# Attention with 64-row products issued in pairs, and the maximum carried in row 64

## The reference

```python
x  = tok_emb + pos_emb                          # layer 0: embedding
h  = x + attn0(layernorm(x))                    # softmax(q k^T / 8) x, no value or output weights
h  = h + ffn0(layernorm(h))                     # one of 16 routed experts plus a shared one, two layers
h  = h + attn1(layernorm(h))                    # with biases, value and output weights
h  = h + ffn1(layernorm(h))                     # 8 experts, the 2 best per token, exact gelu
```

## Time and profile before

| | us |
|---|---|
| median of three runs (934.78 to 936.87) | 935.1 |
| the profiled execution | 936.95 |
| its span, first to last instruction | 935.1 |
| PE busy | 891.6 (95%) |
| weight loads busy | 631.5 (68%) |
| DVE, ACT, POOL busy | 603.8, 576.6, 384.1 |

### The profile page before, as it was taken

The page is one execution under the profiler, slowest core; times in us unless marked ns, Lnnn a source line. Parts: engine busy times, 40 slices in busy tenths (PEclk is TensorE's granted clock), DMA queues, the critical chain, the costliest instruction groups (busy, mean ns, idle before and its releaser), DMA issues.

```text
span 935.1 us, 21847 instructions
## 1 busy us (share of the span) xinstructions
PE 891.6 (95%) x6198; PEld 631.5 (68%) x6198; DVE 603.8 (65%) x2610; ACT 576.6 (62%) x1195; POOL 384.1 (41%) x523
## 2 busy tenths in 40 slices
PE   4879999999999999979999999999999999999998
PEld 2657666666766676656666676666777777777775
DVE  5876777778787899967777777774434343434321
ACT  1336666666666666646666666666666666666664
POOL 0133444444437888834444344443333333333300
PEclk9999999999999999989999999999999999999999
DMA  4000000000001222200000000000000000000000
GB/s 103 2 1 2 1 0 0 0 0 0 1 1 49 72 73 68 75 7 1 1 0 0 0 0 1 1 1 7 12 18 11 17 11 17 11 17 11 18 13 23
DMA packets 18995, 15.13 MB, mean 16 GB/s; under 512 B 5762, under 2 KB 18946, under 8 KB 18946
## 3 DMA queue, kind: packets, MB, share of 16 engines
q1 hardware_dynamic: 18946, 14.52, 5.6%
HBM read 10.32 MB, written 4.19 MB: 16 GB/s over the span
## 4 chain that ended last, share of the span: by engine, by line
PE 83%; DVE 12%; issue 2%; ACT 1%; DMA 1%; DVEq 0%; POOL 0%; SPq 0%; ACTq 0%
PE bank L1226 13%; PE bank L1058 13%; PE bank L1206 7%; PE bank L1024 7%; PE bank L1207 6%; PE bank L971 5%; DVE nmax L743 5%; PE bank L1049 5%; PE bank L1050 5%; PE bank L1135 4%; PE bank L996 3%; PE bank L1037 2%; PE bank L1013 2%; PE bank L1014 2%; PE bank L1003 2%
## 5 line engine op out<-in xcount | busy, mean ns | idle before, releaser
L743 DVE TENSOR_REDUCE nmax<-bank 128x1 fp32r<-128x512 f32 x256 | 170.4, 687 | 47.7 <-PE bank L1024 47.5
L360 POOL TENSOR_TENSOR XS<-XN,XS 128x252 fp32r<-128x252 f32 x128 | 98.0, 765 | 211.6 <-ACT XS L402 211.6
L342 POOL TENSOR_TENSOR rstd<-VE,half 128x4 f32<-128x4 f32 x128 | 129.2, 1009 | 119.6 <-DVE VE L661 119.6
L504 ACT ACTIVATE PT<-bank 128x512 f32<-128x512 f32 x256 | 146.0, 596 | 41.8 <-PE bank L1050 35.5
L354 POOL TENSOR_TENSOR XN<-XC,rstd 128x252 f32<-128x252 f32 x128 | 78.3, 612 | 183.9 <-PE bank L1058 183.7
L556 ACT ACTIVATE PT<-bank 128x512 f32<-128x512 f32 x256 | 132.2, 605 | 3.5 <-PE bank L1207 2.8
L475 ACT ACTIVATE OT<-bank 128x256 f32<-128x256 f32 x96 | 36.8, 384 | 154.3 <-PE bank L1058 103.8
L1058 PE MATMUL bank<-PT,XN 128*64 128x256 f32 x1024 | 124.7, 386 | 0.0
L1226 PE MATMUL bank<-PT,W 128*64 128x256 f32 x1024 | 124.5, 386 | 0.0
L1024 PE MATMUL bank<-X,QH 128*128 128x512 f32 x256 | 108.2, 424 | 8.6 <-DVE nmax L743 1.7
L1049 PE MATMUL bank<-QH,X 128*128 128x512 f32 x256 | 113.1, 442 | 0.5 <-ACT Q L497 0.5
(11 more groups left out here) (136 smaller groups left out, 1506.4 us busy)
## 6 DMA issues: line engine op xcount, KB each, us to landing
WR<-experts SPq DMA_DIRECT2D x64, 129.0 KB, 2.0
out<-H SPq DMA_DIRECT2D x32, 128.0 KB, 1.7
W<-pack SPq DMA_DIRECT2D x5, 252.5 KB, 3.9
W<-pack SPq DMA_DIRECT2D x1, 251.5 KB, 5.1
W<-pack SPq DMA_DIRECT2D x1, 243.0 KB, 5.6
tk<-tokens SPq DMA_DIRECT2D x1, 64.0 KB, 4.4
route_sb<-route SPq DMA_DIRECT2D x1, 0.2 KB
```

The lines of the kernel that those rows point to most:

```text
L342: pl.tensor_tensor(rstd[:, par, :], VE[:, par, :], half[:, :], ALU.pow).then_inc(sigma_done, 1)
L504: sc_.activation(PT[:, par, kt, :], bank[4 + kt % 2][:, :], ACT.Exp, scale=SCALE).then_inc(s.e_ready, 1)
L743: v.tensor_reduce(nmax[:, par, t:t + 1], bank[2 + t % 2][:, :], axis=AX, op=ALU.max, negate=True).then_inc(s.max_ready, 1)
```

## The change

In both attentions the products for the maxima use 64 rows instead of 128: rows 0 to 63 of `QH` against rows 0 to 63 of `X2`. The odd tiles use rows 64 to 127 of `QH` (which holds the projection twice) against a new buffer `XD`, whose rows 64 to 127 are a copy of rows 0 to 63 of `X2`. An even and an odd tile are issued one behind the other (`pair_for_max`). The products with `Q2` are halved in the same way (`low_scores`) and come ahead of those with `QH` (`high_scores`), which stay at 128 rows. Minus the maximum now stands in row 64 of `QH` instead of row 0 of `Q2`; `nmax` is 65 columns wide for that, zero but for the last, `spread_max` writes rows 0 to 64 of bank 0, and the matrices that make the queries have a zero in column 64. ACT fills `XD` behind `X2`, and both are told by one semaphore.

```diff
-            nmax = sb("nmax", [P, 2, NT], F32R)
+            XD = sb("XD", [P, 2, SEQ], F32R)
+            nmax = sb("nmax", [P, 2, NT, D + 1], F32R)
...
-                sc_.activation(X2[:, par, :], bank[0][:, :], ACT.Copy).then_inc(s.x2_ready, 1)
+                ins = sc_.activation(X2[:, par, :], bank[0][:, :], ACT.Copy)
+                if s is a0 or s is a1:
+                    ins = sc_.activation(XD[D:P, par, :], bank[0][0:D, :], ACT.Copy)
+                ins.then_inc(s.x2_ready, 1)
...
-                    sc_.activation(Q2[0:1, par, :], bank[7][0:1, :], ACT.Copy).then_inc(s.m_ready, 1)
+                    sc_.activation(QH[D:D + 1, par, :], bank[0][D:D + 1, :], ACT.Copy).then_inc(s.m_ready, 1)
...
+                def pair_for_max(i, par, t):
+                    if t == 0:
+                        pe.wait_ge(s.qh_ready, i + 1)
+                    if t == 2 or not known(i) or i >= 1:
+                        pe.wait_ge(s.max_ready, i * NT + t)
+                    for own, rows, keys in ((t, slice(0, D), X2), (t + 1, slice(D, P), XD)):
+                        mm(bank[2 + own % 2][:, :], QH[rows, par, own * P:(own + 1) * P], keys[rows, par, :],
+                           start=True, stop=True).then_inc(s.s_ps, 1)
...
                 def spread_max(i, par):
                     pe.wait_ge(s.max_ready, i * NT + NT)
+                    if has(i + 1):
+                        pe.wait_ge(s.x2_ready, i + 2)
...
+                def low_scores(i, par, kt):
+                    pe.wait_ge(s.ql_ready, i + 1)
+                    if kt == 2 or not known(i) or i >= 1:
+                        pe.wait_ge(s.e_ready, i * NT + kt)
+                    for own, rows, keys in ((kt, slice(0, D), X2), (kt + 1, slice(D, P), XD)):
+                        mm(bank[4 + own % 2][:, :], keys[rows, par, own * P:(own + 1) * P], Q2[rows, par, :],
+                           start=True, stop=False)
+                def high_scores(i, par, kt):
+                    pe.wait_ge(s.m_ready, i + 1)
+                    for own in (kt, kt + 1):
+                        mm(bank[4 + own % 2][:, :], X2[:, par, own * P:(own + 1) * P], QH[:, par, :],
+                           start=False, stop=True).then_inc(s.st_ps, 1)
```

More of the change, by code:

```diff
@@ L40 @@
 CENTRE, LOWER, FUSE, FUSED, NORM = 8, 15, 17, 20, 14
-CONSTS = 7
+CONSTS = 8
 HIGHS, LOWS = 5, 6
@@ L333, in _ @@
             pl.memset(f32(XS[:, :, :, 0:1]), 1.0).then_inc(consts_set, 1)
-            pl.memset(f32(XS[:, :, :, D:D + 1]), 0.0).then_inc(consts_set, 1)
+            pl.memset(f32(XS[:, :, :, D:D + 1]), 1.0).then_inc(consts_set, 1)
             pl.memset(R1[:, :], 0.0).then_inc(consts_set, 1)
+            pl.memset(f32(nmax[:, :, :, :]), 0.0).then_inc(consts_set, 1)
             pool.wait_ge(consts_set, CONSTS)
@@ L742, in maxima @@
                         dve.wait_ge(s.s_ps, i * NT + (t + 1))
-                        v.tensor_reduce(nmax[:, par, t:t + 1], bank[2 + t % 2][:, :], axis=AX, op=ALU.max,
+                        v.tensor_reduce(nmax[:, par, t, D:D + 1], bank[2 + t % 2][:, :], axis=AX, op=ALU.max,
                                         negate=True).then_inc(s.max_ready, 1)
@@ L754, in finish @@
                     v.tensor_tensor(hb(i), hb(i), ON[:, :, :], ALU.add).then_inc(s.h_done, 1)
+                maxima(0, 0, range(NT))
                 low_parts(0, 0)
-                maxima(0, 0, range(NT))
                 def body(i, par):
-                    if has(i + 1):
-                        low_parts(i + 1, 1 - par)
-                        maxima(i + 1, 1 - par, range(2))
                     if not known(i) or i >= 1:
@@ L765, in body @@
                     if has(i + 1):
-                        maxima(i + 1, 1 - par, range(2, NT))
+                        maxima(i + 1, 1 - par, range(NT))
+                        low_parts(i + 1, 1 - par)
                     moments_on(s, after, i + 5, 1 - par)
@@ L1014, in project @@
                     mm(bank[1][:, :], AL[:, layer, :], X2[:, par, :], start=False, stop=True).then_inc(s.q_ps, 1)
-                def scores_for_max(i, par, t):
+                def pair_for_max(i, par, t):
                     if t == 0:
                         pe.wait_ge(s.qh_ready, i + 1)
[L1020 to L1025, removed]
+                    if t == 2 or not known(i) or i >= 1:
[3 more added lines that the diff above has]
+                           start=True, stop=True).then_inc(s.s_ps, 1)
@@ L1027, in spread_max @@
                 def spread_max(i, par):
                     pe.wait_ge(s.max_ready, i * NT + NT)
+                    if has(i + 1):
+                        pe.wait_ge(s.x2_ready, i + 2)
+                    else:
+                        pe.wait_ge(after.x2_ready, 1)
                     if known(i) and i == 0:
                         pe.wait_ge(h0_ready if before is None else before.h_done, NSEQ)
-                    if not known(i) or i >= 1:
-                        pe.wait_ge(s.m_ready, i)
@@ L1034, in spread_max @@
-                    if not known(i) or i >= 2:
-                        pe.wait_ge(s.h_done, i - 1)
                     for t in range(NT):
-                        last = mm(bank[7][0:1, t * P:(t + 1) * P], nmax[:, par, t:t + 1],
+                        last = mm(bank[0][0:D + 1, t * P:(t + 1) * P], nmax[:, par, t, :],
                                   IR[:, :], start=True, stop=True)
                     last.then_inc(s.m_ps, 1)
[L1041 to L1050, removed]
+                def low_scores(i, par, kt):
[5 more added lines that the diff above has]
+                           start=True, stop=False)
@@ L1071, in attention @@
                     rest_before()
-                for t in range(NT):
-                    scores_for_max(0, 0, t)
+                for t in (0, 2):
+                    pair_for_max(0, 0, t)
                 def body(i, par, lane):
@@ L1078, in body @@
                         project(i + 1, 1 - par)
[L1079 to L1083, removed]
                     if not known(i) or i >= 1:
                         turn_back(s, before, i - 1, 1 - par)
-                    scores(i, par, 2)
+                    low_scores(i, par, 0)
+                    high_scores(i, par, 0)
                     if has(i + 1):
-                        scores_for_max(i + 1, 1 - par, 1)
-                    scores(i, par, 3)
+                        pair_for_max(i + 1, 1 - par, 0)
+                    turn_on(s, after, i + 2, par)
+                    low_scores(i, par, 2)
+                    high_scores(i, par, 2)
                     if has(i + 1):
-                        scores_for_max(i + 1, 1 - par, 2)
-                        scores_for_max(i + 1, 1 - par, 3)
+                        pair_for_max(i + 1, 1 - par, 2)
                     if not has(i + 1):
@@ L1285, in wide, with once @@
         return np.concatenate([m, m], 1)
+    def once(m):
+        m = wide(m)
+        m[:, D] = 0.0
+        return m
     def led(first, m):
@@ L1291 @@
     none = np.zeros(D, np.float32)
-    put("wq0", wide(led(none, x["L0_attn_Wq"])))
+    put("wq0", once(led(none, x["L0_attn_Wq"])))
     put("wk0", wide(led(none, x["L0_attn_Wk"])))
-    put("wq1", wide(led(x["L1_attn_bq"], x["L1_attn_Wq"])))
+    put("wq1", once(led(x["L1_attn_bq"], x["L1_attn_Wq"])))
     put("wk1", wide(led(x["L1_attn_bk"], x["L1_attn_Wk"])))
@@ L1312 @@
     ct[D, 0] = 1.0
-    put("ct", wide(ct))
+    put("ct", once(ct))
     c0 = np.zeros((P, 2, D + 1), np.float32)
```

## The result

The changed kernel takes 955.2 us (median of four runs, 954.28 to 955.52) against 935.9 us beside it: 1.0205 times the time before, 95% interval 1.0187 to 1.0222. That is 19 us slower where 7 us were forecast. The profiled execution took 955.41 us, its span 953.5 us, 18.4 us more than before.

The account below looks back on a forecast made before the run. PE was taken to bound the attentions, in its own order. Its terms summed to +0.10 us a sequence, +6.4 us for 64; with +1 us, 936.95 became 944.3 us, less 1.85 us: 942 us, range 914 to 970 us.

Parts of the forecast that it names:

- Side by side: Products on two row halves run together on PE, so a pair takes the room of one product, 0.23 us.
- a pair's loads in turn: Rival: a pair's two weight loads follow each other, each pair 0.11 us longer, 28 us more, 970 us; chance 0.12.
- no overlap: Rival: the halves do not run side by side, 0.23 us more a pair, 59 us, 1001 us; chance 0.08.
- Loads hidden behind the other half: Rival: a pair's weights load while the other division streams, four loads of 0.11 us go, 914 us; chance 0.20.
- Nine switches and the loads in the open: On PE, seven more switches, +0.63 us a sequence; six open weight loads, +0.66 us, and two taken at half, +0.10 us.
- The wait for DVE goes: PE's wait for DVE before the last product for the maxima goes, with its open load: -0.37 us a sequence.
- both large terms: The division's switches, loads and saved products, 0.47 us a sequence, and the vanished wait for DVE, -0.37 us.
- Even: no cost by these numbers, but no cover either: At the second low pair, PE arrives as the second exponential ends, 1.65 us after the first high scores start: no wait.
- Together +1 us: First `XD` copy on the path into attention 0, 0.5 us, and each phase's last sequence, 0.3 us each.

Follow-up runs that it names:

- both whole: The changed kernel with all eight products over 128 rows again, its order, pairwise waits and copy into `XD` kept: 941.4 us, 1.0057 of the kernel before.

## Why the prediction was wrong

The direction was right, and so was what the division costs on PE; two other terms were not, and with them the size: 942 us were forecast and 955.2 us measured, inside the range given but with a rise nearly three times the one forecast. By the steps:

- *Side by side.* Right: the starts are within 0.01 us. With it the rivals that need a pair's loads in turn, or no overlap, fall. Loads hidden behind the other half did not show either: the load of each pair starts with its product.
- *Nine switches and the loads in the open.* Right: from a pair to the high scores 0.43 us and between the two high products 0.34 us, as laid out. Undoing the division measured 0.42 us a sequence against the 0.47 us that the switches, loads and saved products came to; the extra product of 64 rows cost 15.8 us more than that of 128, where 15 us were expected.
- *The wait for DVE goes.* Right: the product of the earlier trace rows waits no more. With both whole and its wait taken off a sequence is 6.45 us against 6.76 us before, 0.31 us less, where this term had 0.37 us. So both large terms were some 0.05 us too big, and that their sum, +0.10 us, came out as forecast is in part luck.
- *"Even: no cost by these numbers, but no cover either".* This step failed. The second exponential ended at 202.03, 1.63 us behind the start of the first high scores and nearly as laid out (1.65), but the pair's load started only at 202.14, 0.11 us later; the sum names no time for the way from ACT to PE. PE without a wait would have started the pair 0.20 us behind its last transpose, at 202.08. So the wait is 0.08 us, 5 us in all, near the 6 us at which the prediction had priced 0.1 us more on ACT, and the experiments with whole products showed it growing to 0.39 us as soon as PE comes earlier. A step that comes out even should have been priced with the delay of the signal.
- *"Together +1 us"*, the starts of the two attentions. This failed too: they cost some 6 us: the first two sequences of an attention took 2.8 and 4.4 us more than two later ones, where before it was 0.7 us less and 1.6 us more. The sum takes all 64 sequences at durations of full clock and has nothing for the longer idle time at the starts or for the granted clock there, although it fell to half in the trace before.

Together: 0.10 us x 64 = 6 us as forecast, 0.08 us x 64 = 5 us of waiting, 6 us at the starts, 1 us elsewhere: 18 of the span's 18.4 us.

## What to carry to other kernels

A lone pair of products on half the array's rows was not worth it here: each change between whole and divided costs the switch and a weight load that nothing covers, here 0.25 us for one excursion, more than the 0.23 us that one product of 512 columns takes. Whether a longer run of pairs pays, no run here shows. Before a change in the order of an engine is charged to the operations in it, run the new order with the old operations: here the order alone was a gain, the divided operations and the waits in pairs were the loss, and only their sum was slower. When a layout of waits comes out even, put the signal's delay into it, and look at the granted clock where the pipeline starts.

## What the runs showed of the hardware

- Halves of the rows run side by side like halves of the columns: two products of 64 rows and 512 columns start less than 0.01 us apart, and their weight loads, 128 columns each, run together (0.03 us apart where the pair had waited). The opening load (0.11 us), the columns (0.23 us) and the switch behind them (0.09 us) make 0.43 us.
- The price of a switch is about the same for rows as for columns: into 64 rows 0.08 us (0.38 - 0.30), out of them 0.09 us (0.43 - 0.11 - 0.23), out of column halves 0.09 us. The Trainium skill ("TensorEngine Tiling (Array Packing)", Key Properties) has a change of mode drain the engine and names no price; the runs agree that it costs. Its Theoretical Speedup, up to twice the rate, is what the columns of a pair show, and not what a lone pair takes, 0.43 us against 0.46 us.
- From the end of an activation's record to the start of the weight load that it releases 0.11 us passed (202.03 to 202.14), so in 24 of the 29 sequences of attention 0 past its start that the trace shows whole; in the other five it was 0.05 us.
